# Graph attention on one core: 22 edge tiles gathered as K and V rows instead of as x rows

## What is computed

```
q = (feat @ Wq.T + bq).reshape(n, H, HD)
k = (feat @ Wk.T + bk).reshape(n, H, HD)
v = (feat @ Wv.T + bv).reshape(n, H, HD)
score = jnp.einsum('ehd,ehd->eh', q[edge_dst], k[edge_src])
score = jnp.clip(score / math.sqrt(HD), -10.0, 10.0)
...
alpha = ex / den[edge_dst]
wv = jax.ops.segment_sum(alpha[:, :, None] * v[edge_src], edge_dst, num_segments=n).reshape(n, C)
y = wv @ Wp.T + bp
x = feat + y
h = _layernorm(x, ln_g, ln_b)
h = jax.nn.gelu(h @ W1.T + b1, approximate=False) @ W2.T + b2
return x + h
```

## Time and profile before

| | before |
|---|---|
| median of 3 runs | 1149.14 us (1146.2 to 1150.38) |
| span of the profiled execution | 1484.0 us |
| TensorE matmul busy | 1135.0 us, 76% of the span |
| VectorE busy | 954.9 us, 64% |
| GpSimd busy | 912.0 us, 61% |
| ScalarE busy | 672.3 us, 45% |
| mean granted TensorE clock | 0.837 |
| bytes moved by DMA | 312.25 MB |

### The profile page before, as it was taken

How to read it: one execution, slowest core, us unless ns; L and a number is a source line. 1 busy time by engine, 2 the same in 40 slices (tenths; PEclk the granted TensorE clock), 3 DMA queues, 4 the chain that set the end, 5 groups by cost and what they waited for, 6 DMA issues and landing times.

```text
span 1484.0 us, 26187 instructions
## 1 busy us (share of the span) xinstructions
PE 1135.0 (76%) x6188; PEld 724.7 (49%) x6188; DVE 954.9 (64%) x1539; ACT 672.3 (45%) x1936; POOL 912.0 (61%) x1550
## 2 busy tenths in 40 slices
PE   8956778776977778777866876768877967877887
PEld 6823335454544454444544544544544544544566
DVE  6806676677676576666666666657667657666573
ACT  3212235455544545535544544535544535544543
POOL 4584667677776566766667566666667566666500
PEclk9976668999898788888798788887897788878699
DMA  9985877768777667776677676676677676676510
GB/s 328 314 253 178 254 227 225 229 199 253 214 220 225 203 188 222 227 232 196 197 237 208 191 230 197 199 236 179 206 236 209 191 238 196 197 225 199 180 54 23
DMA packets 154887, 312.25 MB, mean 210 GB/s; under 512 B 32200, under 2 KB 73126, under 8 KB 154791
## 3 DMA queue, kind: packets, MB, share of 16 engines
q0 software_dynamic: 61536, 200.85, 45.6%
q1 hardware_dynamic: 93254, 110.43, 23.3%
HBM read 270.02 MB, written 41.16 MB: 210 GB/s over the span
## 4 chain that ended last, share of the span: by engine, by line
PE 42%; another core or an unknown queue 23%; ACT 14%; issue 14%; DVE 5%; ACTq 1%; DVEq 0%; DMA 0%; SPq 0%
PE bank L483 9%; PE bank L503 7%; PE bank L951 5%; PE quad L875 4%; PE bank L930 3%; PE quad L942 3%; PE bank L977 3%; PE bank L964 2%; ACT hid L496 2%; PE bank L455 2%; ACT hid L491 1%; DVE kv L1636 1%; ACT hn L1276 1%; ACT staged L1217 1%
## 5 line engine op out<-in xcount | busy, mean ns | idle before, releaser
L401 POOL DMA_INDIRECT kv<-kv_rows,src_sb x750 | 721.5, 962 | 443.4 <-PE bank L951 212.1
L1616 DVE TENSOR_TENSOR prod<-kv,quad 128x1024 f32<-128x1024 f32 x196 | 239.3, 1221 | 346.6 <-remote 228.0
L1636 DVE TENSOR_TENSOR kv<-kv,bank 128x1024 f32<-128x1024 f32 x196 | 238.2, 1215 | 16.7 <-ACT kv L1209 16.7
L1623 DVE TENSOR_REDUCE score<-prod 128x32 f32<-128x1024 f32 x196 | 237.7, 1213 | 0.8
L483 PE MATMUL bank<-hT,w_sb 128*128 128x256 f32 x736 | 212.4, 440 | 17.9 <-ACT hid L491 17.9
L951 PE MATMUL bank<-kv,onehot 128*32 128x264 f32 x1568 | 150.1, 442 | 83.2 <-issue 49.5
L503 PE MATMUL bank<-w_sb,hid 128*128 128x256 f32 x736 | 205.3, 435 | 0.9 <-issue 0.7
L483 PEld LDWEIGHTS bank<-hT,w_sb 128*128 128x128 f32 x736 | 159.6, 222 | 52.5 <-issue 11.6
L942 PE MATMUL quad<-qwin,onehotT 32*128 32x256 f32 x1568 | 108.8, 354 | 95.7 <-issue 54.1
L503 PEld LDWEIGHTS bank<-w_sb,hid 128*128 128x128 f32 x736 | 159.8, 223 | 34.5 <-issue 8.7
L930 PE MATMUL bank<-staged,place 128*128 128x264 f32 x196 | 81.5, 502 | 113.8 <-ACT staged L1217 76.0
(11 more groups left out here) (164 smaller groups left out, 1421.0 us busy)
## 6 DMA issues: line engine op xcount, KB each, us to landing
qwin<-q_rows SPq DMA_DIRECT2D x392, 64.0 KB
dst_rows<-edge_dstT SPq DMA_DIRECT2D x50, 256.0 KB
q_rows<-q_next SPq DMA_DIRECT2D x25, 512.0 KB
kv_rows<-kv_out SPq DMA_DIRECT2D x24, 512.0 KB
kv<-kv_rows,src_sb POOLq DMA_INDIRECT x750
agg_rows<-acc_sb SPq DMA_DIRECT2D x98, 82.5 KB
xT_sb<-xT SPq DMA_DIRECT2D x25, 256.0 KB, 5.4
xq_sb<-xT SPq DMA_DIRECT2D x25, 256.0 KB
```

The lines of the kernel that those rows point to most:

```text
L401: return nc.gpsimd.indirect_dma_start(out=rows, out_offset=None, in_=kv_dram, in_offset=bass.IndirectOffsetOnAxis(ap=index, axis=0))
L1616: nc.vector.tensor_tensor(prod[:, slot % 2].rearrange("p (i c) -> p i c", c=C), kv[:, slot, :, 0:C], quad[:, :, 0:C], ALU.mult).then_inc(s ...
L1623: nc.vector.tensor_reduce(score[:, slot % 2], prod[:, slot % 2].rearrange("p (h d) -> p h d", d=HD), AX.X, ALU.add).then_inc(s_score, 1)
L1636: nc.vector.tensor_tensor(kv[:, slot, :, C:2 * C].rearrange("p i (h d) -> p i h d", d=HD), kv[:, slot, :, C:2 * C].rearrange("p i (h d) -> ...
```

## The change

`X_TURN`, the first turn with an x tile in slot 7, becomes the number of turns, and the two functions that ask for it follow:

```diff
@@ -55,7 +55,7 @@
     TURNS = -(-(BATCHES + 3) // SLOTS)
     LOOPED = max(TURNS - 7, 0) // 2
     LOOP_FROM = 6 if LOOPED else TURNS - 1
-    X_TURN = 2 if LOOPED else TURNS
+    X_TURN = TURNS
     X_EARLY = X_FIRST + X_ODD
     X_TILES = [(0, 0, 3), (0, 1, 2), (0, 1, 3)]
     X_TILES += [divmod(2 * p + 5, SLOTS) + (X_TILE,) for p in range(X_ODD)]
@@ -79,7 +79,7 @@
 
 
 def x_turn(turn):
-    return not isinstance(turn, int) or X_TURN <= turn < LOOP_FROM + 2 * LOOPED
+    return X_TURN <= (turn if isinstance(turn, int) else LOOP_FROM) < LOOP_FROM + 2 * LOOPED
 
 
 def x_early(turn, i):
@@ -89,7 +89,7 @@
 
 def x_tiles(turn, i):
     if not isinstance(turn, int):
-        return (X_TILE,) if i == X_SLOT else ()
+        return x_tiles(LOOP_FROM, i)
     return tuple(t for u, b, t in X_TILES if (u, b) == (turn, i))
```

## The result

| | before | after |
|---|---|---|
| median of the runs | 1149.46 us (4 runs, 1146.2 to 1150.38) | 1177.32 us (4 runs, 1173.21 to 1178.42) |
| ratio to before | | 1.0236, interval 1.0209 to 1.0263 |
| span of the profiled execution | 1146.2 us (profiled again, below) | 1176.6 us |

The change makes the kernel slower by 27.9 us, 2.4%; forecast were some 22 us, in a range of 1140 to 1183 us.

The account below looks back on a forecast made before the run. GpSimd's issue rate of gathers was taken as the bound: 1149.1 + 29.1 (added gathers) - 0.5 (setup) - 6.5 (slack given up) = 1171.2, rounded to 1171 us, +1.9%; range 1140 to 1183 us.

Parts of the forecast that it names:

- The floor: Whole kernel before: start 79.6, 750 gathers at GpSimd's pitch 993, landing 5.4 and end 60.8 give at least 1138.8 us.
- 22 x 1.324 = 29.1 us on the path: GpSimd, turns 2 to 23: 22 added gathers and iotas each cost one full pitch, +29.1 us if its queue never waits.
- Slack given up, -6.5 us: GpSimd's queue: of up to 10 us of waiting for buffers, 3 to 4 us kept as consumers get lighter, -6.5 us.
- The setup, -0.5 us: Setup, L820: 22 x gathers fewer, mostly hidden behind the projection; gain between 0 and 2.9 us, taken as 0.5.
- The signs named in advance: Profile after: L401 counts 772, L820 10; L970, L1243, L1257 lose 22 each (L970 44 matmuls); pitch without waits stays 1.32.
- the floor of 1168: Changed kernel: 1138.8 + 29.1 = 1167.9 us; a time below it would mean the pitch in the runs differs from the trace.
- TensorE, ScalarE and the bytes at nothing: Turns: 68 us less TensorE and 30 us less ScalarE hidden behind gather issue, added gather bytes below the pitch; 0 us.
- The waits of the first profile: GpSimd's 212.1 us for free buffers and VectorE's 228.0 us for "remote" were read as mostly the recorded execution's own.
- 329 us of waiting, 335 us between span and median: GpSimd, first to last gather: 1322 us less 993 of issue; removing this waiting from span 1484 was to give median 1149.
- may move either way: Profile after: if GpSimd's idle time before L401 stays above 300 us, the span may rise or fall.
- Rival A: Turns, slot 7: the consumer chain bounds and the x tile stands in it; pitch under 1.300, 1128 us, faster; chance 0.15.

## Why the prediction was right

**The floor, and reading it as the bound: right.** 79.6 + 993 + 5.4 + 60.8 = 1138.8 us was put against the median of 1149. In the profile of the same kernel on a chip of the first kind, the parts are 80.15, 994.55 and 71.5. The 10 us over the floor were not waits of GpSimd, as I had supposed. 5.3 us of them stand behind the last gather, where I had 66.2 us and 71.5 were measured; the 5.4 us that I took for the landing of the last gather were 10.6 up to the last product. 1.5 us more are between the gathers, and 1.9 us lie between the span and the time of the execution.

**22 x 1.324 = 29.1 us on the path: right,** and the part from first to last gather grew by more, 35.3 us. The 6 us beyond it, the long gathers and one wait for a buffer, had no term in the sum.

**Slack given up, -6.5 us: wrong.** There was no slack in the issue. 4.5 us came back behind the last gather, and not through lighter consumers: they come back with the x work kept too, and the profile before has a stretch of low clock there. With 29.2 + 6.1 - 4.5 - 0.4 the spans differ by 30.4, and the medians by 27.9; the forecast had 22. The step that was off is the slack: I took GpSimd's waits to hold 10 us, and they held 1.4. Without this term the sum is 1177.7, and 1177.3 were measured; that this is so near is luck, since 6 us of irregular steps and 4.5 us at the end, neither foreseen, nearly cancel.

**The setup, -0.5 us: right,** -0.4 in the two profiles, which is no more than two profiles may differ by. GpSimd's idle 44.6 us show that the 22 x gathers had been free. The signs named in advance came too: L401 counts 772 and L820 10, L970 has 44 matmuls fewer, and the time lies above the floor of 1168.

**TensorE, ScalarE and the bytes at nothing: right, each by a run of its own** (1.0231 with the work kept; 1.0218 with 181 gathers halved). The queue was busier than I had it beside the issue: 57.0% and 30.1% of the span before, 0.92 from the first gather to the last, yet it was no bound. The Trainium skill, page "DMA: Bandwidth & Descriptors", section "Anatomy of one DMA — SWDGE (gpsimd) path", calls descriptor generation a small, variable part and lets a DMA's cost grow with its bytes. For one transfer's latency no run here speaks to that. For a stream of them these runs do: 0.957 us of the engine at 128 KB and 0.968 at 256 KB, and the stream costs the engine's time.

**The waits of the first profile: wrong explanation, right conclusion.** I read 212 us of waits for buffers and 228 us of "remote" as a product of the recording. They belong to a kind of chip: on it, the runs of this kernel take 1456 to 1491 us. My two numbers that agreed (329 us of waiting, 335 us between span and median) agreed because on the other kind those waits are absent, not because of the recorder. What the prediction said of the profile after ("may move either way") holds for the second kind only. On the first, span and run time differ by under 2 us.

**Rival A, the consumers bound and the x tile stands in their way,** was refuted where the case was timed. On the second kind of chip its sign and nearly its size came out, 18 us faster where it had 21; the size is luck in part, since the 42.5 us behind it come from a trace of that kind and half of them was a guess. I had tied it to a shorter pitch. What differs is that the consumers are slower; the pitch in stretches without waits is 1.325 on both.

What stays open: what slows the second kind. Its traces put it under "remote", an unnamed releaser, on VectorE, ScalarE and GpSimd alike. The issue of eight loads of Q windows in the setup takes 22.66 us there and 4.62 on the first kind:

```profile
88.67 22.66 SPq L624 DMA_DIRECT2D qwin<-q_rows  x8
```

(the queue of SyncE, kernel before, first profile), and profiled again:

```profile
88.90 4.62 SPq L624 DMA_DIRECT2D qwin<-q_rows  x8
```

The register moves beside these loads (MOVE, L624), which take 29 to 42 ns each in the profile again, take 3 to 754 ns in the first. This shows that SyncE's queue is held up too, and not only at its transfers, but not by what.

## What to carry to other kernels

Before trusting the shares of busy time, take an engine's back-to-back pitch from its timeline, gaps included, multiply it by the count of instructions and add what stands before and after. If this comes within 1% of the measured time, that engine is the bound even at 78% busy, and each instruction put on it costs its full pitch. And when the span of a profile and the measured times differ by a quarter, do not explain the waits away: profile again, for what bounds, and with it the sign of a change, may differ from one chip to the next. Here the same edit costs 2.4% on one kind and gains 1.4% on the other.

## What the runs showed that I had not expected

Two kinds of chip (or of their condition) for one program: 1148 us and 1456 to 1491 us, with mean granted TensorE clocks of 0.94 and 0.84 in the profiles before. The lower clock goes along with TensorE's waits there (busy for 76% of the span instead of 88%); which is cause and which effect was not tried.

The time of an indirect DMA on GpSimd, 0.96 us for 128 rows, does not depend on whether a row has 1 or 2 KB (0.957 and 0.968 us on average). Where it was over 1.1 us, in the two profiles compared, an operation L412 or L464 of VectorE was under way in every case when it began. The iota behind it fell from 0.204 to 0.153 us when its columns fell from 64 to 1, and the pitch with it. So 22 gathers more are paid for by 0.055 us less per gather: the changed kernel with the short iota takes 1138.6 us. The kernel before with the short iota, which might be faster still, was only timed on the second kind of chip, where it took 0.4 and 2% longer.
